# Two groups' norm moved into the last MLP, the last scores ahead of the last full output in the wide attention, and the first MLP's weight ordering cut into steps

## The reference, cut to what matters

```python
# layer 0: two wide cross attentions (16 heads of 128, one learned key and value), then an MLP
x = x + cross_attention(layer_norm(x) , ctx, ...)        # attention 1
x = x + cross_attention(layer_norm(x) , ctx, ...)        # attention 2
h = layer_norm(x, ln_mlp_scale, ln_mlp_offset)
x = x + gelu(h @ w_fc1 + b_fc1) @ w_fc2 + b_fc2          # 256 -> 1024 -> 256
# layer 1: grouped cross attention (32 query heads, 8 key heads of 8 features), norm at its end
q = x @ Wq + bq; k = ctx @ Wk + bk; v = ctx @ Wv + bv    # Wq, Wk, Wv, Wo: the weights ordered below
x = layer_norm(x + softmax(q k^T * scale + mask) v @ Wo + bo) * gamma + beta
# layer 2: normed 1x1 convolutions with one attention per sequence
# layer 3: self attention, cross attention (16 heads of 16), then
ln_out = layernorm(x, ln3_s, ln3_b)
return x + gelu_tanh(ln_out @ w1 + b1) @ w2 + b2         # 256 -> 1024 -> 256
```

## Time and profile before

| what | us |
|---|---|
| median of 3 runs | 1762.68 (1760.12 to 1764.04) |
| the profiled execution | 1762.88 |
| span of the profiled execution | 1761.2 |
| mean granted TensorE clock | 0.979 of full speed |
| TensorE busy | 1669.6 (95%) |
| ScalarE busy | 976.3 (55%) |
| VectorE busy | 891.6 (51%) |
| GpSimd busy | 552.1 (31%) |

### The profile page before, as it was taken

How to read it: one execution, slowest core, us unless ns; L and a number is a source line. 1 busy time by engine, 2 the same in 40 slices (tenths; PEclk the granted TensorE clock), 3 DMA queues, 4 the chain that set the end, 5 groups by cost and what they waited for, 6 DMA issues and landing times. The chain is left out here.

```text
span 1761.2 us, 35486 instructions
## 1 busy us (share of the span) xinstructions
PE 1669.6 (95%) x14356; PEld 1436.7 (82%) x14356; DVE 891.6 (51%) x1676; ACT 976.3 (55%) x1862; POOL 552.1 (31%) x602
## 2 busy tenths in 40 slices
PE   7999999999999999999999899899989789988799
PEld 6999999999989999999999788677666567776698
DVE  6533333333444333333333364477859656668532
ACT  4445554555445455455544355477648767776444
POOL 5311000100153010000000162257844468776611
PEclk9999999999999999999999899999989999999799
DMA  5030000000000000000000010210010000001001
GB/s 170 25 124 25 0 24 24 21 2 24 25 1 25 25 1 24 24 24 0 24 24 1 1 31 1 64 43 2 2 23 1 7 1 2 2 7 37 1 13 36
DMA packets 59136, 40.06 MB, mean 23 GB/s; under 512 B 15725, under 2 KB 58262, under 8 KB 59030
## 3 DMA queue, kind: packets, MB, share of 16 engines
q1 hardware_dynamic: 57414, 37.78, 7.3%
q10 hardware_dynamic: 1616, 0.79, 0.2%
HBM read 36.46 MB, written 2.10 MB: 22 GB/s over the span
## 5 line engine op out<-in xcount | busy, mean ns | idle before, releaser
L629 ACT ACTIVATE l0a_q<-l0a_q_ps,l0a_head_bias 128x512 f32<-128x512 f32 x128 | 88.4, 690 | 331.0 <-PE l0a_q_ps L83 331.0
L830 DVE TENSOR_TENSOR l0a_c_lo<-l0a_c_ps,l0a_c_hi 128x512 fp32r<-128x512 f32 x64 | 44.3, 692 | 279.8 <-ACT l0a_c_hi L682 279.8
L326 POOL TENSOR_TENSOR l0a_w_lo<-l0a_raw,l0a_w_hi 128x512 fp32r<-128x512 f32 x32 | 41.7, 1303 | 446.6 <-ACT l0a_w_hi L600 446.6
L840 DVE TENSOR_TENSOR x<-l0a_o_ps,x 128x1024 f32<-128x1024 f32 x64 | 78.3, 1224 | 164.2 <-PE l0a_o_ps L83 127.5
L81 PE MATMUL l0a_v_ps<-l0a_wv_hi,ctx_hi 128*128 128x256 f32 x512 | 150.5, 294 | 0.0
L81 PE MATMUL l0a_o_ps<-l0a_wo_hi,l0a_c_hi 128*128 128x256 f32 x512 | 149.5, 292 | 0.7 <-DVE l0a_c_lo L830 0.7
L82 PE MATMUL l0a_v_ps<-l0a_wv_lo,ctx_hi 128*128 128x256 f32 x512 | 144.5, 282 | 0.0
L82 PE MATMUL l0a_o_ps<-l0a_wo_lo,l0a_c_hi 128*128 128x256 f32 x512 | 144.1, 282 | 0.0
L83 PE MATMUL l0a_o_ps<-l0a_wo_hi,l0a_c_lo 128*128 128x256 f32 x512 | 144.1, 282 | 0.0
L83 PE MATMUL l0a_v_ps<-l0a_wv_hi,ctx_lo 128*128 128x256 f32 x512 | 144.0, 281 | 0.0
L633 ACT ACTIVATE l0a_k<-l0a_kt_ps,l0a_head_bias 128x512 f32<-128x512 f32 x128 | 88.2, 689 | 63.4 <-PE l0a_kt_ps L83 63.0
(11 more groups left out here) (444 smaller groups left out, 4919.8 us busy)
## 6 DMA issues: line engine op xcount, KB each, us to landing
l0a_raw_v<-in_L_xattn_wv_dram SPq DMA_DIRECT2D x16, 256.0 KB, 3.4
l0a_raw_o<-in_L_xattn_wo_dram SPq DMA_DIRECT2D x32, 128.0 KB, 2.8
l3a_room<-in_L_xattn_wo_dram SPq DMA_DIRECT2D x2, 2048.0 KB, 8.9
l0a_raw<-in_L_xattn_wq_dram SPq DMA_DIRECT2D x31, 128.0 KB, 2.3
l0a_raw<-in_L_xattn_wk_dram SPq DMA_DIRECT2D x31, 128.0 KB, 2.3
x<-in_x_dram SPq DMA_DIRECT2D x4, 512.0 KB, 7.8
l3a_room<-in_L_xattn_w_fc_dram SPq DMA_DIRECT2D x2, 1024.0 KB, 6.5
l3a_room<-in_ctx_dram SPq DMA_DIRECT2D x1, 2048.0 KB, 10.7
```

What stands on the lines that cost most here:

```text
L326: return pool.tensor_tensor(w[p][1][:], raw[p][:], w[p][0][:].bitcast(F32), ALU.subtract)
L629: act.activation(q[p][:], q_ps[:], ACT.Identity, bias=head_bias[p][:, 0:1]).then_inc(q_done, 1)
L830: dve.tensor_tensor(c[p][1][:], attended[p][:], c[p][0][:].bitcast(F32), ALU.subtract).then_inc(c_lo, 1)
L840: dve.tensor_tensor(chip.x[:, own, :], o_ps[:], chip.x[:, own, :], ALU.add).then_inc(added, 1)
```

## The change

It has three parts that do not depend on each other.

**The wide attentions' slot 63.** `last_scores(S)` is true for S = 63 alone. There PE makes the scores ahead of the output of the slot, and DVE leaves out the slot's addition; it makes it in slot 64 behind the softmax.

```diff
+        def last_scores(S):
+            return S == ATT * PASSES * NG - 1
...
-                    if prev:
+                    def output():
                         pe.wait_ge(wo_split, i + 1)
...
-                    if this:
+
+                    def score():
                         pe.wait_ge(q_done, heads_before(2))
                         pe.wait_ge(k_done, heads_before(2))
...
+                    if prev and not last_scores(S):
+                        output()
+                    if this:
+                        score()
+                    if prev and last_scores(S):
+                        output()
...
+                    def add_output(u, n):
+                        own = group_rows(u - 1)
+                        dve.wait_ge(o_made, n)
+                        dve.tensor_tensor(chip.x[:, own, :], o_ps[:], chip.x[:, own, :], ALU.add).then_inc(added, 1)
...
+                    if S is not None and S > 0 and last_scores(S - 1):
+                        add_output(u - 1, n - 1)
```

```diff
-                        if turn and g == 1 and f == 2:
-                            hooks["vector_order"](dve)
+                        if turn and g == 1 and f in range(2, 6):
+                            hooks["vector_order"](dve, f - 2)
...
-                            if g == 1 and f == 2:
-                                hooks["scalar"](act)
+                            if g == 1 and f in (3, 7):
+                                hooks["scalar"](act, (f - 3) // 4)
...
-    def scalar(act):
+    def scalar(act, step):
+
         act.wait_ge(raw_in, 64)
-        act.wait_ge(ordered_done, 1)
-        for w_, src in splits:
+        if step == 1:
+            act.wait_ge(ordered_done, 1)
+        for w_, src in splits[2 * step:2 * step + 2]:
```

```diff
-        return t // 2 if t is not None and t % 2 == 1 and (t < TILES - NT or following and t < TILES - GT) else None
+        return t // 2 if t is not None and t % 2 == 1 and (t < TILES - NT or following and t < TILES - 2 * GT) else None
...
+                def normalise_late(n):
+                    own = group_rows(n + 2)
+                    pool.wait_ge(late_gathered, n + 1)
+                    pool.tensor_scalar(late_spread[:], chip.x_moments[:, own, 1], 1e-5, None, ALU.add).then_inc(late_spread_done, 1)
...
-                    if late is not None and f == 0 and isinstance(g, int) and g == NG - 1:
-                        pe.wait_ge(late_lo, CH)
+                    if late is not None and f == 0 and g >= 2:
+                        pe.wait_ge(late_lo, CH * (g - 1))
...
-                        if late is not None and isinstance(g, int) and g == 0 and f == LATE:
-                            turn_late()
+                        if late is not None and g < LATES and f == LATE:
+                            turn_late(g)
...
-                    with act.Fori(1, NG) as g:
+                    for g in range(1, NG):
                         for f in range(FC):
                             chunk(g, f)
+                            if late is not None and g < LATES and f == LATE + 1:
+                                take_late(g)
...
+                        if late is not None and g == 0 and f == 2:
+                            gather_late(1)
```

More of the change, by code:

```diff
@@ L836, in slots @@
                         measure_context(S - 1)
-                    if prev:
-                        own = group_rows(u - 1)
-                        dve.wait_ge(o_made, n)
-                        dve.tensor_tensor(chip.x[:, own, :], o_ps[:], chip.x[:, own, :], ALU.add).then_inc(added, 1)
+                    if prev and not last_scores(S):
+                        add_output(u, n)
                 dve.wait_ge(x_in[0], 16)
@@ L969, in rest_of_entry @@
                                            ALU.subtract).then_inc(x_lo_done, 1)
+                def normalise_late(n):
+                    own = group_rows(n + 2)
+                    pool.wait_ge(late_gathered, n + 1)
+                    pool.tensor_scalar(late_spread[:], chip.x_moments[:, own, 1], 1e-5, None, ALU.add).then_inc(late_spread_done, 1)
+                    pool.wait_ge(late_spread_done, n + 1)
+                    if n > 0:
+                        pool.wait_ge(late_rows_done, GT * n)
+                        pool.wait_ge(late_turned, CH * n)
+                    pool.tensor_tensor(late_inverse[:], late_spread[:], chip.minus_half[:].to_broadcast([P, GT]),
+                                       ALU.pow).then_inc(late_inverse_done, 1)
+                    pool.wait_ge(late_inverse_done, n + 1)
+                    for t in range(GT):
+                        at = own.start + t
+                        pool.tensor_scalar(late_rows[:, t, :], chip.x[:, at, :], chip.x_moments[:, at, 0:1], late_inverse[:, t:t + 1],
+                                           ALU.subtract, ALU.mult).then_inc(late_rows_done, 1)
                 if entry is not None:
@@ L1122, in chunk, with take_late @@
                     act.activation(hidden_hi[f % 2][:], hidden[f % 2][:], ACT.Copy).then_inc(hi_done, 1)
+                def take_late(n):
+                    for c in range(CH):
+                        act.wait_ge(late_turned, CH * n + c + 1)
+                        act.activation(chip.h_hi[:, c, group_columns(n + 2)], late_ps[:, c, :], ACT.Identity,
+                                       bias=late[:, 1, c:c + 1], scale=late[:, 0, c:c + 1]).then_inc(late_hi, 1)
                 def high_weights(f):
@@ L1135, in _ @@
                     if late is not None and f == LATE + 1:
[L1136 to L1139 removed]
+                        take_late(0)
                 if turn:
@@ L1191, in take_whole, with gather_late @@
                                           ALU.mult, ALU.add).then_inc(x_whole_done, 1)
+                def gather_late(n):
+                    own = group_rows(n + 2)
+                    for t in range(own.start, own.stop):
+                        last = dve.bn_aggr(chip.x_moments[:, t, :], chip.x_stats[:, t, :])
+                    last.then_inc(late_gathered, 1)
                 def lows(g, done=None):
@@ L1232, in _ @@
                 if late is not None:
-                    for t in range(last_rows.start, last_rows.stop):
-                        last = dve.bn_aggr(chip.x_moments[:, t, :], chip.x_stats[:, t, :])
-                    last.then_inc(late_gathered, 1)
+                    gather_late(0)
                 if entry is not None:
@@ L1249, in _ @@
                 else:
-                    with dve.Fori(0, NG - 2) as g:
+                    for g in range(NG - 2):
                         between(g)
-                        lows(g + 1, g)
+                        lows(g + 1)
                 between(NG - 2)
```

70 lines of the change are left out of this document (33 added, 37 removed).

## The result

The changed kernel takes 1750.48 us (median of 5, 1749.68 to 1752.18); the kernel before, beside it, 1761.61 (median of 5, 1758.77 to 1764.04). The ratio is 0.993, 95% interval 0.9917 to 0.9944: faster, by 9.9 to 14.6 us. Forecast were 1746.7 and a gain of 16.2. The time lies inside the range (1743 to 1753), 3.8 above the likeliest 1746.7; what the experiments had to find is the 3 to 4 us by which the gain fell short of 16.2. The profiled execution of the changed kernel took 1749.68 (span 1747.4), 13.2 less than the one of before.

The account below looks back on a forecast made before the run. TensorE's work bounds the last MLP; elsewhere its waits and the lowered clock behind them count. Gains of 6.9 + 4.8 + 4.5 = 16.2 against the profiled 1762.88 gave 1746.7 us, range 1743 to 1753.

Parts of the forecast that it names:

- the clock did not stay at half in slot 64: Wide attentions' slot 64: rival that half clock stays, the slot change gives only 3.1, time 1750.5; chance 0.13.
- the score chain did not keep the last attentions: Last two attentions: rival that only the score chain moves, late norm gives 2.2 - 0.9 = 1.3, time 1749.9; chance 0.10.
- layer 1 lost 2 to its clock, not 25: Layer 1: rival that a lower clock makes its work 25 us longer, net 9 slower, 1772; chance 0.03.
- Part A, 6.9 forecast: Wide attentions' slots 63 and 64: 3.1 from the idle time, the rest from full clock; 6.9, bounds 3.1 and 6.9.
- Part B, 4.8 forecast: First MLP's group 1, weights' ordering: wait 3.22 plus 1.55 of a lower-clock chunk; 4.8, bounds 3.2 and 4.8.
- Part C, 5.4 - 0.9 forecast: Last norm moved: 5.4 gained in last two attentions, 0.9 added in last MLP; 4.5, bounds 1.3 and 7.4.
- more than 1 us a sign of being wrong: Last MLP: growth by more than 1 us would show the prediction wrong; 0.9 was expected for eight added transposes.
- two rivals that did not come: Half clock staying in slot 64 (1750.5, chance 0.13) and score chain keeping the last attentions (1749.9, chance 0.10).
- theory one: Experiments' theory, whole kernel: every part gives its waits; the clock decides the rest, differing from execution to execution.
- theory two: Experiments' theory, whole kernel: one part gives less in most executions than in the profiled one.

Follow-up runs that it names:

- the filled slot: The kernel before with 15 matmuls of 128x512 added in slot 64 of the wide attentions, where TensorE waited 3.93 us; ratio 0.9987 to the kernel before.
- after, again: The changed kernel with no edit, measured a second time: 1750.0 us beside 1762.87 for the kernel before, ratio 0.9925.

## Why the prediction was right, and where 3 us of it went

**Mechanisms.** All three parts work where and how the prediction put them: scores at 993.5 (993.8 forecast) and no idle time ahead of slot 64's turning; copies in their room; no row of the turned norm behind, and no late row waited for. None of the rivals came as stated: the clock did not stay at half in slot 64 (stage (2) is 13.39 or 13.40 in nine of nine traces with the new order), the score chain did not keep the last attentions, and layer 1 lost 2 to its clock, not 25. But the reason given against that last rival, that the idle times there are untouched, does not hold as a reason: behind the same barrier (1.96 or 1.97 idle) and the same wait of 2.52 the start of layer 1 took 19.72 to 23.34.

**Part A, 6.9 forecast.** 3.0 are the wait (12.92 to 9.91, in every trace). The rest was taken as 3.8 at full clock. In the profiled execution of before it is 17.00 - 13.39 = 3.6. In the three other traces with the old order it is 2.2, and the time of the filled slot says 2.3. Outside the profiled pair A is worth 5.2 by the stages.

**Part B, 4.8 forecast.** 3.2 are the wait, again in every trace; the 1.55 of the chunk at the lower clock was 1.55 to 1.66 in three executions and 0.14 or 0.15 in two. The mean of stage (3) is 106.45 without B (five traces) and 102.31 with it (seven): 4.1.

**Part C, 5.4 - 0.9 forecast.** Stage (5) is 234.3 without C (mean of four) and 229.4 with it (mean of seven without other edits there): 4.9. In the two profiled executions it is the 5.4 that were worked out from slot 30 to the last tile's turning. The 1.6 behind the wait for the queries goes against it there, and 0.9 come on top behind that turning (10.29 to the last MLP before, 9.35 after), where the prediction let the rest keep its length. In the other traces the last turning comes 4.9 earlier and the rest keeps its length, 9.15 in the mean of either kind. In all eleven other traces with the wait for the queries the first scores behind it took 1.36 to 1.99; before's 1.09 was the exception. The last MLP grew by 1.1 in the mean (87.95 to 89.04), 0.95 in the profiled pair. The prediction called more than 1 us a sign of being wrong; this is at that mark, but TensorE's waits in the stage are the same in both (2.0 and 0.2), and the traces of one kind spread as much (87.36 to 88.44 without C).

**Sum.** 5.2 + 4.1 + 4.9 - 1.1 = 13.1, where the two comparisons gave 12.3 and 13.2. This leaves out stage (4). With the 1.9 by which its two groups of traces differ it is 11.2, which the intervals (9.9 to 14.6 and 10.8 to 15.7) hold as well, so the times don't say whether that loss belongs to the change.

What was mis-sized is the same kind of term in A and B: the rows at half clock behind a wait, read from a single execution, were taken in as if the whole of their excess came back each time. That is 1.6 too much in A (17.00 in the profiled execution, 15.63 in three others) and 0.7 in B (1.55, but 0.14 or 0.15 in two traces of five); C's 5.4 was 0.5 too high. The bounds held all of it (3.1 to 6.9, 3.2 to 4.8, 1.3 to 7.4), but I took the upper end twice. In the profiled pair itself A and B gave 6.6 and 5.05, nearly what was forecast. What that pair is short of was lost in two places that the sum didn't look at: 2.1 at layer 1's start and 1.6 behind the wait for the queries. So theory one holds for the waits, and theory two for A, whose gain is 1.4 less outside the profiled pair.

That the time still fell inside the range is in part luck: the high end, 1753, had been set for two rivals that did not come, and it is this room that took up the 3 to 5 us.

The Trainium skill, "TensorE: Matmul & The Clock Gate", What's actually happening, says that the activity monitor runs freely, so that one kernel shows different numbers of slow matmuls. The traces agree: at layer 1's start the first three groups of scores of one and the same kernel took 1.99, 1.99 and 1.38 in after, and 1.09, 1.99 and 1.67 in after, again. The prediction cited this for A's new order, where it changed nothing; it bore on the size of what the old order lost.

**Not settled:** what decides, in an execution, how much of layer 1's start runs at half clock, and whether two or more of the parts together make it more. And the single parts' times have intervals of 3 to 5 us, so their sizes rest on the traces.

## What to carry to other kernels

Split a gain at an idle TensorE into the wait, which repeats to a few hundredths, and the half-clock rows behind it, which differed by 1.4 us and more between executions; count the first in full and the second between nothing and what the one trace shows. Allow as much again for stages behind the change that have waits of their own, as layer 1 does here. Matmuls into a free bank inside a wait that can't be removed show what the clock costs there (2.3 us in the wait of 3.93; in the one of 2.52 they held the clock too, but no gain in time was shown). An engine that finishes a low part nobody wants yet, ahead of a short result that TensorE waits for, is worth reordering, but look for what then stands behind it.

## What the runs showed of the hardware

Waits of 0.82, 0.84, 0.61 and 0.30 within 12 us left the granted clock at 1.00 in slot 64 (nine of nine traces with the new order), and one of 3.93 or 3.94 was followed by half clock in four of four with the old order. Between them it differs. Behind the wait of 3.06 or 3.07 in the first MLP the next chunk was 1.55 to 1.66 longer in three of five traces, and in the two others 0.14 and 0.15 longer. Behind the 2.52 at layer 1 the next scores ran at 1.98 or 1.99 in four of the twelve unfilled traces and at 1.09 in eight, but in seven of these eight the second group took 1.92 or 1.99; with the wait filled, all groups ran at 1.09, in two of two. Keeping TensorE busy in slot 64 cost nothing else: the 15 extra matmuls took 3.77 inside a wait of 3.93, 0.25 of it was left, and stage (1) stayed at 12.93.

VectorE's low part of 128x512 took 2.33 in after while POOL's mask addition ran (2.37 for 128x1024), where it takes both operands from SBUF (`l3a_whole`, `h_hi`); where one of them came from PSUM (`l3a_turn_value_ps`) it took 0.69 beside the same addition, as at 1450.12:

```profile
1450.12 0.69 DVE L1984 TENSOR_TENSOR h_lo<-l3a_turn_value_ps,h_hi 128x512 fp32r<-128x512 f32 x1 [1.53 <-ACT h_hi L1860]
```

```profile
1449.98 2.39 POOL L1619 TENSOR_TENSOR l3a_room<-l3a_room,l3a_mask_bias 128x1024 f32<-128x1024 f32 x1
```

The bias copy of 1x256, on a single partition, took 1.38 in before while POOL formed a low part, and 0.28 in after, at 1051.01, while POOL took an inverse of 128x4. That neither the shape nor the partition count, but the neighbour, made it long was not tested by a run of its own.
